# The first token tile of layer two built from a gather and a product of slots and tokens

## The chip, the cores and the metric

One core of one Trainium2 chip. The metric is the device time of one launch in microseconds; the time quoted for the kernel before is the median of three runs.

## What is computed

There are 4096 tokens (128 samples of 32 tokens) of 256 features. Layer one adds to `x` a mixture of four experts over a per-sample mixed input. Each expert takes its 1024 best tokens, runs a two-layer network over them, scales each row by its probability and adds it to that token's row. Layer two is a gated network with low-rank adapters that the sample's subject selects, followed by one more linear layer, again added to its input.

```python
# layer one (x_mixed = x @ cond_weights[subject])
for i in range(E):                                    # E = 4, capacity = 1024
    score = where(assigned_i, probs[:, i], -inf)
    sel_p, sel_idx = top_k(score, capacity)
    h = gelu(flat_x[sel_idx] @ W1[i])
    out = out.at[sel_idx].add(h @ W2[i] * p)          # scatter-add of rows
x = x + out
# layer two: y = x@W + (x@A[subject])@B[subject] for gate, up and down
h = silu(lora(x, Wg, Ag, Bg)) * lora(x, Wu, Au, Bu)
x = x + lora(h, Wd, Ad, Bd) @ (weight * scale).T + bias
```

## The kernel before

Every fp32 matrix is split into two fp32r parts, hi and lo, and a product is three matmuls (`product`, L1081 to L1083).

**Layer one** runs in 8 blocks of 512 slots, two blocks for each expert. A block has 8 steps of the hidden dimension. A step `s` is an up-product into `bank[s % 2]`, two gelus on ACT (`hid`, L564; `hf`, L567), one subtraction on DVE (`hid_lo`, L957) and, two steps later on PE, a down-product that accumulates the block's rows in PSUM. The last block, number 7, is cut into two parts of 256 slots, 8 steps each; its four quarters of 128 rows stand in banks 4 to 7. ACT scales the finished rows by the slot's probability (`rows_of_y`, L554) and POOL adds them to the token rows `x1_rows` in HBM by an indirect DMA with addition (`scatter`, L452), four for each block. A block's scatters wait for those of the block before.

**The order of layer two's tiles** is computed on chip: samples are sorted by subject so that each tile of 16 samples (512 tokens) needs two adapters. A product with `sample_id` and `goes_is` gives the order; DVE reads it in step LAST0+8 (`sample_rows`, L938 and L941), writing `sample_at` (the sample at each place) and `x1_row` (row numbers for the gathers) and raising `ids_in` to 5.

**Between the layers** stands the part that the change touches. PE finishes block 7 (`down(STEPS0 - 1, split=True)`), then runs 40 matmuls that nobody reads (`keep_busy(WAIT_X1, ...)`, L1175), and waits for the rows of tile 0. ACT splits off the first adapter pair's columns (`adapter_columns`, L597 and L600), then scales the last two quarters of block 7 and loads the Silu table. POOL scatters these quarters; when all scatters have landed (`scattered`), SP and ACT each read one quarter of tile 0 (`first_rows`, L341), and POOL the other two (`gather_x1(0)`, L480) and then tile 1. PE turns the four quarters of `x1_sb[0]` (L1344), ACT takes `x1s_hi` (L631), DVE `x1s_lo` (L999), and PE begins tile 0: eight matmuls that need the hi part only (L1352, L1353), the low-rank products (L1260, L1262), the rest of the first two hidden steps, and the adapter products (L1293).

**Layer two** then runs in 8 tiles of 512 tokens, 8 hidden steps each. In step 3 of each tile PE turns the rows of the next one (L1254). POOL gathers the adapter rows `b_pair` (L472) and the token rows, one tile or two ahead. The outputs are stored by SP.

Each engine has its own queue of instructions in program order. POOL's indirect DMAs share one DMA queue.

## Time and profile before

| what | value |
|---|---|
| median of three runs | 651.91 us (651.81 to 652.7) |
| the profiled execution's own time | 653.1 us |
| its span, first to last instruction | 651.3 us |
| PE, matmul busy | 605.0 us (93%) |
| PE weight load busy | 503.4 us (77%) |
| DVE busy | 382.1 us (59%) |
| ACT busy | 214.4 us (33%) |
| POOL busy | 132.6 us (20%) |
| mean granted clock of TensorE | 0.971 |

The engines are PE (TensorE matmul), PEld (its weight load), DVE (VectorE), ACT (ScalarE), POOL (GpSimd) and SP (SyncE). The span is what the trace covers. Layer one ends and layer two begins between 277 and 302 us of the span. A granted clock of 1.00 is the level of 2.4 GHz, 0.50 the level of 1.2 GHz.

### The profile page before, as it was taken

The page shows a single profiled execution, that of the slowest core. Times are in us where ns is not written, and L with a number is a line of the kernel's source. Part 1 is how long each engine was busy: PE and PEld are TensorE (multiplying, and loading weights), DVE is VectorE, ACT ScalarE, POOL GpSimd, SP SyncE. Part 2 cuts the span into 40 slices and gives each one's busy share as a digit, 9 for nine tenths or more (in the row PEclk, how much of TensorE's full clock was granted, in tenths as well). Part 3 has the DMA queues.
Part 4 walks back from the last instruction along what each step waited for, and adds up shares of the span by engine and source line. Part 5 has one row for each costly group of instructions (what it writes and reads, how often), then busy time and mean ns, then how long its engine had stood idle before and what let it go on. Part 6 is the DMA issues. An engine that isn't in the chain of part 4 may idle for free.

```text
span 651.3 us, 9696 instructions
## 1 busy us (share of the span) xinstructions
PE 605.0 (93%) x3323; PEld 503.4 (77%) x3323; DVE 382.1 (59%) x827; ACT 214.4 (33%) x448; POOL 132.6 (20%) x113
## 2 busy tenths in 40 slices
PE   4867389999999999979999999999999999999994
PEld 2735269999999999967888888888888888888883
DVE  7687867886786556505455545554555455545533
ACT  2435025764874755432212213122122131221110
POOL 4000040745453540652002003011030020000000
PEclk9979579999999999999999999999999999999997
DMA  8996329416329330831003104013031040120012
GB/s 309 318 334 234 106 87 365 65 36 192 34 78 295 42 49 9 195 70 45 0 1 117 21 1 126 13 41 96 2 117 21 0 125 12 45 61 2 13 21 33
DMA packets 64219, 60.74 MB, mean 93 GB/s; under 512 B 37424, under 2 KB 56624, under 8 KB 62832
## 3 DMA queue, kind: packets, MB, share of 16 engines
q1 hardware_dynamic: 53072, 38.04, 19.2%
q0 software_dynamic: 8736, 21.76, 13.5%
q10 hardware_dynamic: 2368, 0.39, 0.3%
q8 instruction: 23, 0.38, 0.2%
q14 instruction: 20, 0.16, 0.1%
HBM read 44.98 MB, written 19.40 MB: 99 GB/s over the span
## 4 chain that ended last, share of the span: by engine, by line
PE 86%; DVE 7%; DMA 2%; issue 1%; ACT 1%; POOL 0%; SPq 0%; ACTq 0%; DVEq 0%; POOLq 0%
PE bank L1081 23%; PE bank L1082 22%; PE bank L1083 22%; PE bank L1293 5%; PE bank L1262 3%; PE bank L1260 3%; DVE mix_row L668 2%; PE bank L1140 1%; PE bank L1114 1%; PE bank L1147 1%; PE bank L1194 1%; DVE onehot_r L831 1%; PE bank L1254 1%; DVE passed L780 1%; DVE passed_n L783 1%
## 5 line engine op out<-in xcount | busy, mean ns | idle before, releaser
L621 ACT ACTIVATE act<-bank 128x512 f32<-128x512 f32 x64 | 38.2, 598 | 229.9 <-PE bank L1293 229.9
L1046 DVE TENSOR_TENSOR prod<-bank,act 128x512 f32<-128x512 f32 x64 | 44.2, 690 | 99.6 <-PE bank L1293 99.6
L957 DVE TENSOR_TENSOR hid_lo<-hf,hid_hi 128x512 fp32r<-128x512 f32 (+1 forms) x72 | 45.4, 631 | 48.6 <-ACT hf L567 48.2
L1081 PE MATMUL bank<-w_hi,hid_hi 128*128 128x256 f32 x256 | 72.2, 282 | 0.0
L1082 PE MATMUL bank<-w_lo,hid_hi 128*128 128x256 f32 x256 | 72.1, 282 | 0.0
L1083 PE MATMUL bank<-w_hi,hid_lo 128*128 128x256 f32 x256 | 71.5, 279 | 0.0
L452 POOL DMA_INDIRECT x_rows<-y_sb,slot_row x32 | 53.7, 1678 | 65.9 <-ACT y_sb L554 58.9
L564 ACT ACTIVATE hid_hi<-bank 128x512 fp32r<-128x512 f32 (+1 forms) x72 | 39.8, 552 | 71.1 <-PE bank L1083 70.7
L472 POOL DMA_INDIRECT b_pair<-b_rows,b_row x8 | 8.5, 1059 | 238.2 <-PE bank L1312 237.6
L1081 PE MATMUL bank<-xs_hi,w_hi 128*128 128x512 f32 (+1 forms) x144 | 54.7, 380 | 0.0
L1082 PE MATMUL bank<-xs_lo,w_hi 128*128 128x512 f32 (+1 forms) x144 | 53.2, 370 | 0.0
L1083 PE MATMUL bank<-xs_hi,w_lo 128*128 128x512 f32 (+1 forms) x144 | 53.2, 370 | 0.0
L441 POOL DMA_INDIRECT xg<-flat_rows,slot_row x32 | 32.8, 1024 | 91.5 <-DVE slot_row L840 63.7
L1081 PE MATMUL bank<-x1s_hi,wg_hi 128*128 128x512 f32 x126 | 50.5, 401 | 0.9 <-DVE prod L1046 0.9
L1082 PE MATMUL bank<-hid_lo,wd_hi 128*128 128x512 f32 x128 | 50.8, 397 | 0.0
L1081 PE MATMUL bank<-hid_hi,wd_hi 128*128 128x512 f32 x128 | 50.6, 395 | 0.0
L1081 PEld LDWEIGHTS bank<-w_hi,hid_hi 128*128 128x128 f32 x256 | 48.1, 188 | 2.4
L1082 PEld LDWEIGHTS bank<-w_lo,hid_hi 128*128 128x128 f32 x256 | 48.1, 188 | 2.2
L1083 PE MATMUL bank<-hid_hi,wd_lo 128*128 128x512 f32 x128 | 49.8, 389 | 0.0
L1082 PE MATMUL bank<-x1s_lo,wg_hi 128*128 128x512 f32 x126 | 49.3, 392 | 0.0
L1083 PE MATMUL bank<-x1s_hi,wg_lo 128*128 128x512 f32 x126 | 49.2, 390 | 0.0
L1082 PE MATMUL bank<-x1s_lo,wu_hi 128*128 128x512 f32 x126 | 49.0, 389 | 0.0
(262 smaller groups left out, 1299.8 us busy)
## 6 DMA issues: line engine op xcount, KB each, us to landing
w_raw<-in_L_ffn_W SPq DMA_DIRECT2D x8, 1024.0 KB, 7.3
xT<-in_xT SPq DMA_DIRECT2D x8, 512.0 KB, 8.5
x_sb<-in_x SPq DMA_DIRECT2D x8, 512.0 KB, 8.7
flat_rows<-flat_st SPq DMA_DIRECT2D x8, 512.0 KB, 5.5
outT<-out_sb SPq DMA_DIRECT2D x120, 32.0 KB, 1.6
b_rows<-b_all_hi SPq DMA_DIRECT2D x1, 1152.0 KB, 9.4
b_rows<-b_all_lo SPq DMA_DIRECT2D x1, 1152.0 KB, 12.5
wdT<-in_wdT SPq DMA_DIRECT2D x1, 1024.0 KB, 5.3
```

The source lines that it names most:

```text
L441: pool.indirect_dma_start(out=xg[:, q, :], out_offset=None, in_=flat_rows[:, :], in_offset=bass.IndirectOffsetOnAxis(ap=slot_row[:, e, hal ...
L452: pool.indirect_dma_start(out=x1_rows[:, :], out_offset=bass.IndirectOffsetOnAxis(ap=slot_row[:, e, half * GB + q:half * GB + q + 1], axis=0),
L564: act.activation(hid[s % 4][0][:, n], bank[s % 2][:, n], ACT.Gelu)
L621: act.activation(act1[h % 2][:, :], bank[h % 2][:, :], ACT.Silu).then_inc(silu1, 1)
L957: dve.tensor_tensor(lo[:, n], hf[s % 2][:, n], hi[:, n].bitcast(f32), ALU.subtract).then_inc(hid0, 1)
L1046: dve.tensor_tensor(prod[h % 2][:, :], bank[2 + h % 2][:, :], act1[h % 2][:, :], ALU.mult).then_inc(prod1, 1)
L1081: pe.matmul(out, lh, rh, start=start, stop=False, skip_group_check=True)
L1082: pe.matmul(out, lh, rl, start=False, stop=False, skip_group_check=True)
L1083: return pe.matmul(out, ll, rh, start=False, stop=stop, skip_group_check=True)
L1260: pe.matmul(out[:, :], a_pair[par][:, i, :, :].rearrange("p a r -> p (a r)"), hi, start=start, stop=False, skip_group_check=True)
L1262: return pe.matmul(out[0:96, :], a_pair[par][:, i, 0:3, :].rearrange("p a r -> p (a r)"), lo, start=False, stop=stop, skip_group_check=True)
L1293: pe.matmul(out[:, :], b_pair[par][:, i * HID + h * P:i * HID + (h + 1) * P], u[:, :], start=False, stop=True, skip_group_check=True).then ...
```

## The change

Tile 0 of layer two is no longer read after all the scatters have landed. POOL gathers its rows earlier, into `x1_first`, when blocks 0 to 6 have landed, so without block 7. PE turns them between the last two down-products of layer one. Block 7's scaled rows are also kept on chip as hi and lo parts (`y_last`), and DVE writes a 0/1 matrix `pick` with one row for each slot of block 7 and one column for each token of tile 0: 1 where the slot holds that token. Sixteen matmuls of `y_last` with `pick` give block 7's share of tile 0, and DVE adds it to the turned rows. Block 7 is still scattered, for the tiles after the first. The adapter columns of tile 0 move into the last steps of layer one, the 40 matmuls and `first_rows` go, and the Silu table is loaded later.

```diff
@@ SBUF @@
+        x1_first, x1T_first = sb("x1_first", [P, GB, D], f32), sb("x1T_first", [P, KD, BT], f32)
+        first_id, slot_f = sb("first_id", [P, SB, 32], f32), sb("slot_f", [P, GB], f32)
...
+        pick = sb("pick", [P, GB, BT], f32r)
+        y_last = two("y_last", [P, GB, D])
@@ sync @@
-            first_rows(sp, 0)
@@ gpsimd @@
+            pool.wait_ge(ids_in, 5)
+            pool.wait_ge(xsT, KD * NB0)
+            pool.wait_ge(scattered, 16 * GB * (NB0 - 1))
+            for q in range(GB):
+                pool.indirect_dma_start(
+                    out=x1_first[:, q, :], out_offset=None, in_=x1_rows[:, :],
+                    in_offset=bass.IndirectOffsetOnAxis(ap=x1_row[:, q:q + 1], axis=0)).then_inc(first_in, 16)
             pool.wait_ge(b_out, 32)
             pool.wait_ge(packed_in, 1)
             for t in range(2):
                 gather_b(t)
+            pool.wait_ge(first_in, 16 * GB)
             scatter(NB0 - 1)
             pool.wait_ge(scattered, 16 * GB * NB0)
-            pool.wait_ge(ids_in, 5)
-            for t in range(2):
-                gather_x1(t)
+            gather_x1(1)
@@ scalar @@
+            def last_hi(q):
...
+                act.activation(y_last[0][:, q, :], y_at(NB0 - 1, q), ACT.Copy,
+                               scale=slot_p[:, E - 1, GB + q:GB + q + 1]).then_inc(y_hi, 1)
...
                 if h == 1 and part:
                     rows_of_y(b, (0, 1))
+                    for q in range(2):
+                        last_hi(q)
...
+                if s == LAST0 + KH + 3:
+                    act.wait_ge(packed_in, 1)
+                    act.wait_ge(lo1, len(SPLITS1))
+                    adapter_column(0, 0, 0)
+                if s == LAST0 + KH + 5:
+                    adapter_column(0, 0, 1).then_inc(a_in, 1)
...
-            act.wait_ge(lo1, len(SPLITS1))
-            adapter_columns(0, 0, (packed_in, 1))
+            for q in range(2, GB):
+                last_hi(q)
+            act.wait_ge(y_lo, GB)
             rows_of_y(NB0 - 1, (2, 3))
-            act.activation(warm[:, :], cols[:, 0:1], ACT.Silu)
-            first_rows(act, 1)
...
             for k in range(KD):
-                act.wait_ge(x1_t, k + 1)
-                act.activation(x1s[0][0][:, k, :], bank[4 + k][:, :], ACT.Copy).then_inc(x1_act, 1)
-            for k in range(KD):
-                act.wait_ge(x1_lo, k + 1)
-                act.activation(x1T[0][:, k, :], bank[4 + k][:, :], ACT.Copy)
+                act.wait_ge(x1_sum, k + 1)
+                act.activation(x1s[0][0][:, k, :], x1T[0][:, k, :], ACT.Copy).then_inc(x1_act, 1)
+            act.activation(warm[:, :], cols[:, 0:1], ACT.Silu)
@@ vector @@
+            def first_tokens():
+
+                dve.wait_ge(ids_in, 5)
+                dve.tensor_copy(slot_f[:, :], slot_row[:, E - 1, GB:2 * GB])
+                link(dve.scalar_tensor_tensor(first_id[:, :, :], over(sample_at[:, 0:SB], 32), 32.0,
+                                              iota[:, 0:32].unsqueeze(1).to_broadcast([P, SB, 32]), ALU.mult, ALU.add))
+
+            def picked(q):
+
+                dve.tensor_scalar(pick[:, q, :], first_id[:, :, :].rearrange("p s n -> p (s n)"), slot_f[:, q:q + 1], None,
+                                  ALU.is_equal).then_inc(pick_in, 1)
+
+            def last_lo(q):
+
+                dve.wait_ge(y_hi, q + 1)
+                dve.scalar_tensor_tensor(y_last[1][:, q, :], y_at(NB0 - 1, q), slot_p[:, E - 1, GB + q:GB + q + 1],
+                                         y_last[0][:, q, :].bitcast(f32), ALU.mult, ALU.subtract).then_inc(y_lo, 1)
...
+                if s == LAST0 + KH + 1:
+                    first_tokens()
+                if s in (LAST0 + KH + 2, LAST0 + KH + 3):
+                    for q in range(2):
+                        picked(2 * (s - LAST0 - KH - 2) + q)
+                if s == LAST0 + KH + 4:
+                    for q in range(2):
+                        last_lo(q)
...
             for k in range(KD):
-                x1_low(0, k + 1, k, bank[4 + k][:, :])
+                dve.wait_ge(x1_t, k + 1)
+                dve.tensor_copy(x1T_first[:, k, :], bank[2 + k][:, :]).then_inc(first_ev, 1)
+            for q in range(2, GB):
+                last_lo(q)
+            for k in range(KD):
+                dve.wait_ge(pick_mm, k + 1)
+                dve.tensor_tensor(x1T[0][:, k, :], bank[2 + k][:, :], x1T_first[:, k, :], ALU.add).then_inc(x1_sum, 1)
+            for k in range(KD):
+                x1_low(0, k + 1, k, x1T[0][:, k, :])
@@ tensor @@
             down(STEPS0 - 2)
+            pe.wait_ge(ids_in, 5)
+            pe.wait_ge(first_in, 16 * GB)
+            for k in range(KD):
+                for c in range(GB):
+                    last = pe.transpose(bank[2 + k][:, c * P:(c + 1) * P].bitcast(f32r),
+                                        x1_first[:, c, k * P:(k + 1) * P].bitcast(f32r), ident_r[:, :])
+                last.then_inc(x1_t, 1)
             down(STEPS0 - 1, split=True)
...
             pe.wait_ge(lo1, len(SPLITS1))
-            keep_busy(WAIT_X1, bank[0], wg)
-
-            for c in range(GB):
...
+            def from_last(k):
+
+                for q in range(GB):
+                    for j in range(2):
+                        q_, j_ = (q, j) if q < 2 else (2 + j, q - 2)
+                        if k == 0:
+                            pe.wait_ge(y_lo if j_ else y_hi, q_ + 1)
+                        last = pe.matmul(bank[2 + k][:, :], y_last[j_][:, q_, k * P:(k + 1) * P], pick[:, q_, :],
+                                         start=q == 0 and j == 0, stop=q == GB - 1 and j == 1, skip_group_check=True)
+                last.then_inc(pick_mm, 1)
+
+            pe.wait_ge(pick_in, GB)
+            pe.wait_ge(first_ev, KD)
+            for k in range(KD):
+                from_last(k)
```

## Rows read from the trace of the kernel before

**Rows 1.** Chain of waits that ended last, 262 to 302 us: start, us, what.
```profile
281.93 3.78 DMA x_rows<-y_sb,slot_row
...
287.92 2.86 DMA x_sb<-x_rows
...
291.69 0.61 ACT x1s_hi L631
```
**Rows 2.** Busy time of each engine by stretch; then PEclk, DMA share, GB/s.
```profile
288.00:290.80 2.80, 0.03 (x1) 0.00 (x0) 0.00 (x0) 0.00 (x0) 2.15 (x3) 1.00 0.63 171
...
292.30:296.20 3.90, 3.86 (x10) 2.99 (x11) 1.29 (x2) 1.67 (x3) 2.96 (x4) 0.56 0.36 101
...
301.00:303.30 2.30, 1.41 (x7) 0.85 (x6) 0.80 (x2) 1.08 (x2) 0.00 (x0) 1.00 0.00 0
```
**Rows 3.** Timeline of PE: start, us, instruction, [idle before <-releaser].
```profile
277.97 0.34 PE L1081 MATMUL bank<-w_hi,hid_hi 128*128 128x256 f32 x1
...
278.73 9.29 PE L1175 MATMUL bank<-wg_hi 128*128 128x512 f32 x40
...
295.62 0.63 PE L1260 MATMUL bank<-x1s_hi,a_pair 128*128 128x512 f32 x1
...
301.34 0.39 PE L1293 MATMUL bank<-ug,b_pair 128*128 128x512 f32 x1
...
313.48 0.46 PE L1254 MATMUL bank<-ident_r,x_sb 128*128 128x128 f32 x4
```
**Rows 4.** Timeline of POOL, scatters (L452) and gathers (L472, L480).
```profile
264.43 1.56 POOL L452 DMA_INDIRECT x_rows<-y_sb,slot_row  x1 [0.30 <-issue]
...
267.62 1.20 POOL L472 DMA_INDIRECT b_pair<-b_rows,b_row  x1 [0.30 <-issue]
...
285.98 1.02 POOL L480 DMA_INDIRECT x_sb<-x_rows,x_row  x1 [2.49 <-DMA x_rows<-y_sb,slot_row]
...
297.33 0.95 POOL L480 DMA_INDIRECT x_sb<-x_rows,x_row  x1 [0.30 <-issue]
```
**Rows 5.** DMA issues, 262 to 300 us: last number is median us to landing.
```profile
x_sb<-x_rows,x_row POOLq DMA_INDIRECT x10, 2.7
...
x_rows<-y_sb,slot_row POOLq DMA_INDIRECT x7, 3.8
b_pair<-b_rows,b_row POOLq DMA_INDIRECT x2, 7.2
```
**Rows 6.** Timeline of ACT in the last steps of layer one.
```profile
269.06 0.84 ACT L554 ACTIVATE y_sb<-bank,slot_p 128x256 f32<-128x256 f32 x2
...
275.33 0.39 ACT L564 ACTIVATE hid_hi<-bank 128x256 fp32r<-128x256 f32 x1 [0.75 <-PE bank L1083]
...
276.75 0.39 ACT L564 ACTIVATE hid_hi<-bank 128x256 fp32r<-128x256 f32 x1 [0.75 <-PE bank L1083]
277.03 0.38 ACT L567 ACTIVATE hf<-bank 128x256 f32<-128x256 f32 x1
277.67 0.68 ACT L597 ACTIVATE a_pair<-a_all_hi 128x576 fp32r x1 [0.27 <-issue]
...
280.18 1.28 ACT L606 ACT_TABLE_LOAD   x1
```
**Rows 7.** Timeline of DVE in the same steps.
```profile
268.11 1.08 DVE L941 TENSOR_SCALAR x_row<-bank,pack_f 32x32 int32<-32x32 f32 x4
...
277.44 0.42 DVE L957 TENSOR_TENSOR hid_lo<-hf,hid_hi 128x256 fp32r<-128x256 f32 x1 [0.99 <-ACT hf L567]
```
**Rows 8.** Groups by line and shape, DVE and ACT: count | busy, mean ns.
```profile
L1050 DVE CAST hid_hi<-prod 128x512 fp32r<-128x512 f32 x64 | 27.3, 427 | 2.9
...
L994 DVE TENSOR_TENSOR um<-bank,pack_f 128x512 f32<-128x512 f32 x16 | 11.1, 691 | 16.6 <-PE bank L1262 16.6
...
L1010 DVE SCALAR_TENSOR_TENSOR ug<-um_hi,pack_f,um 128x512 fp32r<-128x512 f32 x8 | 6.0, 752 | 0.3
...
L572 ACT ACTIVATE wg_hi<-wg_lo_raw 128x512 fp32r<-128x512 f32 x4 | 2.5, 634 | 0.0
```

## What the change should do to the time

> **What bounds the kernel now.** The chain of waits comes first, because it says what the end of the run hangs on between the layers. PE's work carries it up to the last scaled rows of layer one. Then it leaves PE: the last scatter of block 7 takes 3.78 us to land, the read of tile 0's rows 2.86 us more, ACT's hi part 0.61 us [rows 1]. The timeline of PE shows the same from the other side [rows 3]. The last down-product starts at 277.97, and the 40 matmuls that nobody reads run from 278.73 for 9.29 us, so until 288.0. Then the stretch table has PE at 0.03 of 2.80 us [rows 2], and the low-rank products of tile 0 start only at 295.62. From 277.97 to 295.62 are 17.65 us in which the only useful PE work is one down-product (six matmuls, 277.97 to 278.73, 0.76 us), eight transposes and eight matmuls. The idle stretch has a second price: the granted clock, at 1.00 until then, averages 0.56 from 292.30 to 296.20 [rows 2], so for most of these 3.9 us it is at the 1.2 GHz level. After 295.62 PE is the bound again, so what is gained here should arrive at the end one for one.
>
> **The change, part by part.** I follow the new path with the old times as anchors.
>
> *The early read.* It needs block 6's last scatter, issued at 264.43 [rows 4] and landed 3.8 us later [rows 5], at 268.2, and the row numbers, which DVE finishes at 268.11 + 1.08 = 269.2 [rows 7]. The ten L480 issues start 285.98 to 297.33, 1.26 us apart [rows 4]. So POOL issues the four gathers at 269.3, 270.6, 271.8 and 273.1, and with 2.7 us to landing [rows 5] the last is there at 275.8. With the 3.8 us of a scatter as the upper bound it is 276.9. PE wants them when it has done the last but one down-product, at 277.97. So the read costs nothing; its cover is PE's own work, with 1.1 to 2.2 us to spare. Past that, each microsecond costs one, because the last down-product is queued behind the wait.
>
> *What POOL does later.* The two `b_pair` gathers (before, the second started at 267.62 [rows 4]) now come after the four, at 274.4 and 275.7, and land 7.2 us later [rows 5], at about 283. The first adapter product wants them near 291.7. Then POOL waits for `first_in` (275.8 to 276.9, no real wait) and issues block 7's scatters. Such issues stand 1.56 + 0.30 = 1.9 us apart [rows 4]; the two last quarters now also wait for ACT, which takes them after `y_lo`, and go out at about 281.2 and 283.1, landing at 286.9. Tile 1's four gathers are issued from 287.0 and the last lands at 287.0 + 3 x 1.26 + 2.7 = 293.5. PE turned them at 313.48 [rows 3]; 9.6 us earlier is 303.9. This has 10 us of cover. SP loses `first_rows` and gains nothing.
>
> *ACT.* A step takes 1.42 us (275.33 to 276.75) and two gelus end 0.66 us after its start (276.75 to 277.41) [rows 6], so a step leaves 0.75 us. Two `last_hi` cost as much as the two scaled rows at 269.06, 0.84 us. An adapter column costs 0.27 us before it and 0.68 us for its hi copy [rows 6]; its smaller lo copy has no row here and takes no longer than the hi copy, so 1.0 to 1.6 us, and I take 1.1. Each of these three insertions makes the next gelu 0.3 to 1.0 us late, and the step after catches up, since they sit one or two steps apart. PE takes a step's hidden part two steps later, at which point it has about 1.2 us to spare. Zero, with at most 0.3 us left over at the last but one step.
>
> *DVE.* `first_id` has two broadcast inputs: 0.75 us, as L1010 [rows 8]. The four `picked` have no row of their own. They read one SBUF tile and write one of 512 columns. The nearest row is the cast L1050 with 0.43 us, the upper bound L1010 with 0.75 us [rows 8]. I take 0.45. Two in a step with the 0.42 us of `hid_lo` [rows 7] make 1.3 us, inside a step of 1.42. At 0.75 they make 1.9 us, twice, and PE would stand about 0.6 us. The Trainium skill, "VectorE: DVE Perf Modes", section "The perf-mode tier table", gives `tensor_scalar` on fp32 in SBUF twice the rate of a two-tensor operation, which agrees with L1050 against L1010 and would put the picks at the lower end.
>
> *The new path on PE.* Eight transposes: four take 0.46 us with their drain [rows 3], about 0.3 us each four when they follow each other, so 0.6 us, to 278.55. The last down-product, 0.76 us, to 279.3. DVE copies the turned rows out of PSUM from 278.5 on, two at the 0.69 us of L994 [rows 8], to 279.9, and PE waits for both: 0.6 us idle. The first four products need quarters 0 and 1, long done. ACT's hi parts of quarters 2 and 3 (0.42 us each, from 279.1) are there at 279.9, DVE's lo parts (0.45 each, from 279.9) at 280.8, before the seventh and eighth product ask for them at 281.3. Sixteen products at 9.29 / 40 = 0.23 us [rows 3] are 3.7 us, to 283.6, with the last result at 283.75. Then the sum for the second half on DVE 0.69 us, its hi part on ACT 0.63 us (from SBUF, as L572 [rows 8]), to 285.1, the lo part on DVE 0.69 us, to 285.8. With some 0.2 us for hand-overs the low-rank products start at 286.0. PE has its eight hi matmuls beside this: four from 283.6, four from 285.1, done at 286.0 too.
>
> *What is late next.* The low-rank start moves from 295.62 to 286.0, **9.6 us earlier**. The adapter pair's columns are ready at about 276. The Silu table (1.28 us [rows 6]) is loaded from 285.1 to 286.6, and the first Silu follows L1293, at 301.34 before and about 291.7 after. Nothing else lies between. The two first low-rank matmuls were still at the low clock, another 0.2 to 0.3 us, which I leave as a margin for hand-overs.
>
> *The clock.* PE's idle stretches become 0.6 us and 0.6 us. At 301.00 to 303.30 the kernel before has PE idle for 0.9 us with a granted clock of 1.00 [rows 2]; so I take full clock through the seam. That is part of the 9.6 us: in the stretch at 0.56 the ten matmuls filled 3.9 us [rows 2], and at 0.23 us each they would take 2.3.
>
> **The sum.** The span is 651.3 - 9.6 = 641.7 us. The profiled execution takes 1.8 us more than its span, 653.1, so 643.5 for it; against the median of the runs, 1.2 us under that execution, 651.91 - 9.6 = **642.3 us**.
>
> **The rivals.**
> 1. *The first rows come late* (13%), because DVE's new work holds up POOL's issues. The picks fall at 272 to 274, over the last two gathers. If each pick stopped POOL for its own 0.45 us, four would move the last landing by 1.8 us, to 277.6, and with the 3.8 us of a scatter [rows 5] to 278.7: 0.7 us of stall. With picks of 0.75 us it is 279.9 and 1.9 us of stall. So 643.0 to 644.2. For it: one `b_pair` issue took 1.20 us [rows 4] while DVE wrote the row numbers from 268.11 on [rows 7]. Against it: the gather issued at 297.33 took 0.95 us. The Trainium skill, "SBUF — State Buffer", section "Who interferes with whom", speaks for this rival: it says that a DVE cast or `tensor_scalar` in a two-port mode and GpSimd lock each other out for a whole instruction, so that a DMA from the GpSimd queue waits for its descriptors. No row here shows such a wait alone.
> 2. *The clock falls for a while* (10%). With the 40 matmuls gone, PE's work from 279 to 286 is broken by waits. Half clock over a stretch like the one before, 3.9 us at 0.56, costs 2 us: 644.3.
> 3. *DVE or ACT falls behind in the last steps* (5%): the picks at 0.75 us and the adapter columns at the wrong moment, 0.6 to 1 us: 643.1.
> 4. *Slower than before* (2%): the clock falls and does not come back while PE's work is in pieces. Each microsecond at 1.2 GHz costs half. It eats the whole gain from 19 us at half clock on, and makes the kernel measurably slower from 22 us on; low from 280 to 305 gives 642.3 + 12.5 = 654.8. Against it: it came back within 4 us before [rows 2], behind a longer pause.
> 5. *It doesn't do what it says* (2%): the read waits for block 7 somehow, or the rows land at 287 and PE's last down-product behind them: near 651.9.
>
> **How the numbers follow.** The forecast has 68%. It covers 641.5 (copies and sums faster than L994 says, up to 0.8 us) to 643.2 (picks at the upper bound, some hand-overs). The range of 641.3 to 644.8 adds rivals 2 and 3 and most of 1. A change under 0.2%, 1.3 us, can't be told from none. Faster by more: 0.96, all cases but 4 and 5; within 0.2%: 0.02; slower: 0.02.
>
> **What would show it.** In the profile after: L1175 with WAIT_X1 gone; the transposes of `x1_first` straight behind the last but one down-product, without an idle time released by a DMA; the sixteen products starting near 279.9 at 0.23 us each; the low-rank products near 286.0; PEclk at 1.00 from 278 to 292; tile 1's turn without a wait on a DMA. The prediction is wrong if PE waits for `x1_first` for over a microsecond, if the stretch 279 to 292 has a clock under 0.9, or if the shift at L1293 is not found at the end of the span.

## The result, and the profile after

The changed kernel ran in five of seven jobs; a job is a row of runs on one chip, with runs of the kernel before among them. What the change gives depends on the job. The distance in the table is from the start of the row-number product (L1302 after, in step LAST0+8) to the first adapter product (L1357 after, L1293 before, [rows 3]), in the job's profile. It leaves out what lies ahead of the change, where single executions of any kernel here differ by up to 3 us.

| job | changed, us | before, us | ratio, 95% | distance, us |
|---|---|---|---|---|
| 1 | 647.68 (645.59 to 648.58) | 652.32 | 0.9913 (0.9895 to 0.993) | 29.60 |
| 3 | 643.05 (642.69 to 643.34) | 652.18 | 0.9859 (0.9833 to 0.9884) | 26.80 |
| 4 | 643.39 (642.39 to 644.24) | 654.13 | 0.9834 (0.9814 to 0.9854) | 26.02 |
| 5 | 642.75 (642.43 to 644.79) | 653.26 | 0.9853 (0.9823 to 0.9883) | 26.07 |
| 6 | 643.71 (643.4 to 644.3) | 652.28 | 0.9862 (0.9825 to 0.9899) | 26.04 |

Before, the distance was 35.50. The forecast was 642.3 in a range of 641.3 to 644.8. Job 1, the measurement that it was made for, lies 5.4 us above the forecast and 2.9 us outside its range: half of the gain came. In jobs 3 to 6 all 16 executions are inside. The document has to explain two things: why jobs 3 to 6 came out as they did, and where 4.5 us went in job 1.

**The ordinary profile** is that of job 6 (span 641.6 us). Timeline of PE, start, us, instruction, [idle before <-releaser], as in [rows 3]:

```profile
266.19 0.23 PE L1302 MATMUL bank<-goes_is,sample_id 128*128 128x128 bf16 x1
...
278.32 0.81 PE L1308 MATMUL bank<-ident_r,x_first 128*128 128x128 f32 x8
278.96 0.35 PE L1138 MATMUL bank<-w_hi,hid_hi 128*128 128x256 f32 x1
...
280.36 0.47 PE L1410 MATMUL bank<-pick,y_last_hi 128*128 128x512 f32 x1 [0.46 <-DVE x1T_first L1112]
...
284.09 0.39 PE L1422 MATMUL bank<-x1s_hi,wg_hi 128*128 128x512 f32 x1
...
285.70 0.50 PE L1422 MATMUL bank<-x1s_hi,wg_hi 128*128 128x512 f32 x1 [0.54 <-ACT x1s_hi L656]
...
286.73 0.40 PE L1324 MATMUL bank<-x1s_hi,a_pair 128*128 128x512 f32 x1
```

The turned rows follow the last but one down-product without a pause, the sixteen products start 2.0 us later, and PE stands only twice, for half a microsecond each. The stretch table ([rows 2] has its columns) shows the clock at its upper level throughout, over the 6.4 us of the seam too:

```profile
278.00:280.30 2.30, 1.90 (x19) 1.69 (x17) 1.71 (x4) 0.72 (x2) 2.00 (x2) 1.00 0.98 409
280.30:286.70 6.40, 5.80 (x24) 4.54 (x25) 3.34 (x6) 3.26 (x6) 4.38 (x3) 1.00 1.04 266
286.70:292.00 5.30, 5.30 (x25) 4.21 (x24) 3.65 (x6) 0.45 (x2) 2.43 (x3) 1.00 0.20 45
```

**The profile of job 1** (span 645.6 us), the same timeline:

```profile
277.38 0.28 PE L1140 MATMUL bank<-xs_hi,w_lo 128*128 128x256 f32 x1
...
278.09 0.28 PE L1140 MATMUL bank<-w_hi,hid_lo 128*128 128x256 f32 x1
281.44 0.39 PE L1138 MATMUL bank<-w_hi,hid_hi 128*128 128x256 f32 x1 [3.07 <-issue]
...
284.32 0.47 PE L1410 MATMUL bank<-pick,y_last_hi 128*128 128x512 f32 x1 [0.43 <-DVE x1T_first L1112]
```

PE stands for 3.07 us before a down-product. Its operand was late, and ACT's timeline shows why the operand was:

```profile
273.77 0.39 ACT L587 ACTIVATE hid_hi<-bank 128x256 fp32r<-128x256 f32 x1
...
275.98 0.39 ACT L587 ACTIVATE hid_hi<-bank 128x256 fp32r<-128x256 f32 x1 [1.54 <-PE bank L1140]
...
277.20 0.35 ACT L578 ACTIVATE a_pair<-a_all_lo 128x192 fp32r x1
280.27 0.38 ACT L587 ACTIVATE hid_hi<-bank 128x256 fp32r<-128x256 f32 x1 [2.72 <-remote]
...
281.75 0.38 ACT L587 ACTIVATE hid_hi<-bank 128x256 fp32r<-128x256 f32 x1 [0.82 <-remote]
```

ACT had nothing to do and waited for up-products that PE had long dispatched. The last matmul of the up-products started at 272.97, 274.38, 275.79 and 277.38. In the steps just before them the semaphore rises 0.29 us after such a start. For these four it rises at 273.75, 275.95, 280.25 and 281.73: 0.5, 1.3, 4.2 and 4.1 us later than that. ACT's and DVE's own signals came at once. The profile can't name what ACT waited for, hence "remote"; the chain of waits has the same gap:

```profile
277.20 0.35 ACT a_pair L578
277.55 2.69 another core or an unknown queue
...
280.93 0.80 another core or an unknown queue
```

I call this late signals. The profile of job 1 also lacks some 770 of about 6460 semaphore records.

The last block is not the only place. The same profile has the same signal late in the first step of two earlier blocks, near 135 and 159 us, long before the burst, the early reads, the adapter columns or the matrices. PE and ACT in job 1:

```profile
133.10 0.98 PE L1240 MATMUL bank<-slotted,onehot_r 128*128 128x48 bf16 x32
...
135.17 0.39 PE L1140 MATMUL bank<-xs_hi,w_lo 128*128 128x512 f32 x1
...
137.03 0.60 ACT L587 ACTIVATE hid_hi<-bank 128x512 fp32r<-128x512 f32 x1 [2.45 <-PE bank L1140]
```

and in job 6:

```profile
134.76 0.39 PE L1140 MATMUL bank<-xs_hi,w_lo 128*128 128x512 f32 x1
...
135.19 0.60 ACT L587 ACTIVATE hid_hi<-bank 128x512 fp32r<-128x512 f32 x1 [1.02 <-PE bank L1140]
```

From matmul to gelu it is 1.86 us in job 1 and 0.43 in job 6. PE did not stand there, so this lateness of 1.4 us cost nothing.

### The profile page after: what moved, and what is told of

It is laid out like the page before. It is cut to its first block, busy times and chain, and to the rows that moved or that the text cites. A ratio compares the mean times of both kernels' runs of the same rounds, so it can differ in the third digit from the quotient of the medians.

```text
span 645.6 us, 9619 instructions
## 1 busy us (share of the span) xinstructions
PE 599.7 (93%) x3299; PEld 498.4 (77%) x3299; DVE 388.9 (60%) x841; ACT 214.9 (33%) x450; POOL 134.9 (21%) x115
## 4 chain that ended last, share of the span: by engine, by line
PE 87%; DVE 5%; DMA 2%; issue 1%; ACT 1%; SPq 1%; another core or an unknown queue 1%; POOL 0%; DVEq 0%; ACTq 0%; POOLq 0%
PE bank L1138 23%; PE bank L1139 23%; PE bank L1140 23%; PE bank L1357 5%; PE bank L1326 3%; PE bank L1324 3%; DMA xT<-in_xT 2%; PE bank L1197 1%; PE bank L1171 1%; PE bank L1204 1%; PE bank L1251 1%; DVE onehot_r L854 1%; SPq L363 1%; PE bank L1318 1%; PE bank L1410 1%
## 5 line engine op out<-in xcount | busy, mean ns | idle before, releaser
L452 POOL DMA_INDIRECT x_rows<-y_sb,slot_row x32 | 53.7, 1679 | 62.5 <-ACT y_sb L560 54.9
L472 POOL DMA_INDIRECT b_pair<-b_rows,b_row x8 | 8.2, 1022 | 229.7 <-PE bank L1376 229.1
L1138 PE MATMUL bank<-x1s_hi,wu_hi 128*128 128x512 f32 x126 | 49.0, 389 | 0.0
```

The costliest lines, as they stand in the source:

```text
L452: pool.indirect_dma_start(out=x1_rows[:, :], out_offset=bass.IndirectOffsetOnAxis(ap=slot_row[:, e, half * GB + q:half * GB + q + 1], axis=0),
L1138: pe.matmul(out, lh, rh, start=start, stop=False, skip_group_check=True)
```

## The experiments

Theory 1: the burst of the two `b_pair` gathers (2.36 MB, now issued behind the early reads, 276 to 285 us) falls on layer one's last steps and stalls them. Theory 2: ACT's adapter columns do it. Theory 3: DVE's matrices do. Theory 4: PE's fetch of instructions is held up. After the first runs came theories 5 (transfers and new work together), 6 (the early reads) and 7 (the recording of the execution).

**Job 2: four edits of the changed kernel.**

> POOL issues the two b_pair gathers ahead of the four early reads of x1_first, as it did in the kernel before; nothing else is changed. In the changed kernel PE stands from 278.1 to 281.4 us and again for 1 us behind the gelus of the last two steps, and ACT waits there for signals of PE that come 0.5 to 4 us after PE's own stamps. Theory 1 (the 2.36 MB of b_pair, which now flow from 276 to 284 us, hold up PE's last steps or its signals): the burst ends near 277, the idle 3.07 us goes, and the time falls by 3 to 4 us, to 643.5 to 645. Theory 2 (ACT's adapter columns with their register loads): unchanged at 647.4, stall at the same step. Theory 3 (DVE's picks and lo rows): unchanged. Theory 4 (the block of instructions that PE fetches at 280.6 is held up behind the transfers): falls as under theory 1, with the fetch back at about 277. A new cost in all of them: the early read starts one to two us later if the gathers ahead of it wait.

```diff
+            pool.wait_ge(b_out, 32)
+            pool.wait_ge(packed_in, 1)
+            for t in range(2):
+                gather_b(t)
             pool.wait_ge(ids_in, 5)
...
-            pool.wait_ge(b_out, 32)
-            pool.wait_ge(packed_in, 1)
-            for t in range(2):
-                gather_b(t)
```

> ACT makes the first adapter pair's columns behind the last scaled rows, as before, and no longer between the gelus of layer one's last steps. Theory 2 (the columns with their register loads hold up ACT and with it PE): the idle 3.07 us of PE goes, and the columns lie beside PE's products after 284, so 643.5 to 645. Theories 1 and 4 (transfers): the stall stays at 278 to 281.5, the time at 647.4 within 1 us. Theory 3 (DVE): also unchanged.

```diff
-                if s == LAST0 + KH + 3:
...
-                    adapter_column(0, 0, 0)
-                if s == LAST0 + KH + 5:
-                    adapter_column(0, 0, 1).then_inc(a_in, 1)
...
             for q in range(2, GB):
                 last_hi(q)
+            act.wait_ge(lo1, len(SPLITS1))
+            adapter_columns(0, 0, (packed_in, 1))
```

> DVE makes the four 0/1 matrices and the first two lo parts of the last block's rows behind the copies of the turned rows, no longer between the hidden parts of the last steps. That puts 4 x 0.45 us + 2 x 0.45 us on the path to the sixteen products, 2.5 to 2.7 us. Theory 3 (DVE's work inside the steps makes the stall of 4 us): the idle time of PE at 278 goes and the time is 646 to 647, about the same as the changed kernel. Theories 1, 2 and 4: the stall stays and the time is 649.5 to 650.5.

```diff
-                if s in (LAST0 + KH + 2, LAST0 + KH + 3):
...
-                        last_lo(q)
...
+            for q in range(GB):
+                picked(q)
-            for q in range(2, GB):
+            for q in range(GB):
                 last_lo(q)
```

> POOL issues the two b_pair gathers behind the scatters of the last block, at about 284 us instead of 275.7, so no burst lies over layer one's last steps; its data are needed by the adapter product near 296 us. Theories 1 and 4 (transfers over the last steps): PE's idle 3.07 us at 278 goes, the seam is done near 286, and the adapter products then wait for b_pair (landing near 292 to 293), so 643.5 to 646. Theories 2 and 3 (ACT's or DVE's new work in the steps): the stall stays and the time is 647.4 or more.

```diff
-            pool.wait_ge(b_out, 32)
-            pool.wait_ge(packed_in, 1)
-            for t in range(2):
-                gather_b(t)
             pool.wait_ge(first_in, 16 * GB)
             scatter(NB0 - 1)
+            pool.wait_ge(b_out, 32)
+            pool.wait_ge(packed_in, 1)
+            for t in range(2):
+                gather_b(t)
             pool.wait_ge(scattered, 16 * GB * NB0)
```

| kernel, job 2 | us | ratio, 95% | distance, us |
|---|---|---|---|
| `b_pair` first | 644.71 (643.44 to 646.35) | 0.9858 (0.9829 to 0.9886) | 26.96 |
| columns late | 647.39 (646.93 to 647.79) | 0.9906 (0.9878 to 0.9933) | 30.40 |
| picks late | 650.79 (649.13 to 651.89) | 0.9961 (0.9946 to 0.9977) | 33.28 |
| `b_pair` last | 644.16 (643.36 to 647.11) | 0.987 (0.9832 to 0.9907) | 26.81 |

The changed kernel did not run in this job; the measure is its 29.60 us of job 1. With the burst moved away, to either side, the 3 us go. With ACT's or DVE's work moved away they stay: theories 2 and 3, as the sole cause, fall. PE's and ACT's rows with `b_pair` last:

```profile
275.04 0.39 ACT L587 ACTIVATE hid_hi<-bank 128x256 fp32r<-128x256 f32 x1 [1.56 <-PE bank L1140]
...
277.68 0.38 PE L1138 MATMUL bank<-w_hi,hid_hi 128*128 128x256 f32 x1 [0.25 <-DVE hid_lo L998]
```

The signals still begin to be late at the same step, by up to 1.35 us, but they recover at once. Theory 4 falls by the kernel with the columns late: PE's block of instructions is fetched at 275.9 there (276.2 in the kernel before), and ACT's longest wait comes after it:

```profile
279.30 0.38 ACT L587 ACTIVATE hid_hi<-bank 128x256 fp32r<-128x256 f32 x1 [2.30 <-remote]
```

In that kernel, and in the one with the picks late, the clock fell behind the stall, which is my rival 2 as a follower of something else. With the columns late the sixteen products then take 5.17 us (282.45 to 287.62) instead of 3.73 (stretch table, columns late):

```profile
278.00:280.00 2.00, 1.21 (x13) 1.06 (x11) 0.01 (x1) 0.66 (x2) 1.70 (x2) 1.00 1.04 410
280.00:282.00 2.00, 0.97 (x6) 0.77 (x6) 1.51 (x3) 0.84 (x2) 0.54 (x1) 1.00 0.94 327
282.00:284.00 2.00, 1.55 (x4) 1.29 (x5) 0.98 (x3) 1.59 (x4) 0.00 (x0) 0.51 1.04 279
```

**Job 3: parts alone in the kernel before, and the changed kernel again.**

> This is the kernel before with POOL's order of the changed kernel alone: four early reads of x1_first (into a tile that nobody reads), then the two b_pair gathers, then block 7's scatters. ACT, DVE and PE do what they did. The changed kernel's stall over the last steps is measured by the signals of PE: they come 0.3 us behind the last matmul's start until 272 us and 0.5 to 4.2 us late after it. Theory 1 (the transfers alone do it): PE's last down-products are 3 to 4 us late, as in the changed kernel, and the time is 655 to 656.5. Theory 5 (only the transfers together with the new work of ACT and DVE in the same steps): PE runs through its last steps without idle time, and the time is 653 to 654, the 1 us being the later scatters.

> The kernel before with the two b_pair gathers issued when PE has done all but three down-products of layer one, near 275 us, between the two halves of block 7's scatters, so that the burst of 2.36 MB lies where the changed kernel has it; there are no early reads. Theory 1 in its narrow form (the burst over the last two steps does it, whoever else is at work): PE stands for 2 to 4 us before its last two down-products, 655 to 656.5. Theory 4 (a fetch of instructions, which PE makes at 276.2 us in the kernel before, is held up behind the burst): the same, with the fetch seen 2 to 4 us later. Theory 6 (the early reads are needed for the stall): no idle time on PE, at most 1 us from scatters that go out beside the burst, 652 to 654.

```diff
                 for q in range(GB):
+                    if b == NB0 - 1 and q == 2:
+                        pool.wait_ge(b_out, 32)
+                        pool.wait_ge(packed_in, 1)
+                        pool.wait_ge(down0, STEPS0 - 3)
+                        for t in range(2):
+                            gather_b(t)
                     pool.wait_ge(y_out, GB * b + q + 1)
```

> The changed kernel with the b_pair gathers behind the scatters, and with DVE's 0/1 matrices and first lo parts and ACT's adapter columns all taken out of the last steps, so that of the change only the early reads and ACT's two hi parts are left in them. There PE's signals were still up to 1.35 us late with the b_pair gathers alone taken away. If that rest comes from ACT's and DVE's new work, PE's signals are on time (0.3 us) and the last down-product but one starts 0.7 us earlier; if it comes from the early reads, the lateness stays. Either way the 2.7 us of DVE's work now lie on the path: 646 to 647.5, against 644.2 with them in the steps.

> The changed kernel itself once more, beside the others. If the stall is a property of the program, PE stands again for 3 us before its last down-product but one and ACT's last two hidden parts wait for PE's signals; the distance from the start of the row-number product to the first adapter product is 29.6 us again (35.5 in the kernel before), and the time 646.5 to 648.5. If it was one execution's accident, the distance is near 27 us.

The first kernel takes POOL's lines of the change as they stand, the third joins the edits of three kernels above. Measured: reads in the kernel before 656.8 us (654.33 to 658.94), 1.0069 (1.0048 to 1.009); burst late 655.79 (654.9 to 658.66), 1.006 (1.0032 to 1.0088); steps free 646.98 (645.9 to 647.99), 0.9916 (0.9886 to 0.9945), distance 29.24; the changed kernel 643.05, distance 26.80. The two edits of the kernel before have distances of 38.29 and 37.98, against 35.50.

Nobody's signals were late in this job. Theory 1 as I had put it falls here: the changed kernel has its burst in the same place and no stall. Both edits of the kernel before are slower, but not by PE's steps, in which ACT's idle time stays at 0.67 to 0.75 us. By the time alone theory 1 (655 to 656.5) would have seemed right for both. They are slower since tile 0 waits there for block 7's scatters, and these are now issued behind or beside the burst. Timeline of POOL with the burst late, the last scatter and what waited for it:

```profile
281.36 1.57 POOL L458 DMA_INDIRECT x_rows<-y_sb,slot_row  x1 [0.30 <-issue]
287.37 1.02 POOL L486 DMA_INDIRECT x_sb<-x_rows,x_row  x1 [4.45 <-DMA x_rows<-y_sb,slot_row]
```

The chain of waits has its landing:

```profile
281.36 5.76 DMA x_rows<-y_sb,slot_row
```

That is 5.76 us, against 3.78 in [rows 1]. With the early reads the last scatter is issued 1.4 us later and lands in 4.09 us. The rest of the 2.8 and 2.5 us of distance goes with the clock, which is at 0.50 for 6.8 us behind the wait in both and for 3.4 us in the kernel before. The medians are 4.6 and 3.6 us slower; what lies beyond the distance I have not traced. So the changed order of POOL is bearable only with the rest of the change.

In the changed kernel PE waited for the first rows in this job. It turns them 12.82 us behind the row-number product, in job 6 12.13 us behind it, and these 0.69 us are nearly all of the difference between 26.80 and 26.04:

```profile
278.18 0.86 PE L1308 MATMUL bank<-ident_r,x_first 128*128 128x128 f32 x8 [0.53 <-DMA x_first<-x_rows,x_row]
```

The chain of waits shows why: the last of the four reads took 4.87 us from issue to landing, where I had taken 2.7 and at most 3.8.

```profile
273.18 4.87 DMA x_first<-x_rows,x_row
```

**Job 4: side by side, on the chip of job 2.**

> The changed kernel a third time, as the measure for the three beside it. Its two profiles so far differ: in one PE's signals to ACT came up to 4.2 us late over the last steps of layer one, PE stood for 3 us, and the runs gave 645.6 to 648.6; in the other, taken on another chip, they were on time and the runs gave 642.7 to 643.3. If the lateness belongs to the chip, this run and the three beside it show one of the two throughout; if it belongs to the single execution, the runs of one kernel scatter between 643 and 648.

> The two b_pair gathers behind the last block's scatters, as in an earlier run, now beside the changed kernel on the same chip. Where PE's signals are late, the theory that the b_pair burst stretches the lateness says 3 us less than the changed kernel beside it, with at most 1.4 us of lateness left. Where they are on time, the two kernels are within 1 us.

> As the kernel beside it with the b_pair gathers last, and with DVE's 0/1 matrices and first lo parts and ACT's adapter columns out of the last steps. It pays 2.7 us for that. If the late signals come from the work of ACT and DVE in these steps, they are on time here and late in the other three; if from the early reads, they are late by up to 1.4 us here too; where the chip shows no lateness at all, the distance from the row-number product to the first adapter product is 29.2 us again.

> The kernel with the b_pair gathers last, its four early reads left out: x1_first is filled with zeros by one instruction on POOL in their place, so the first tile lacks what the rows would bring. ACT's and DVE's new work stays in the steps. If the early reads make PE's signals late, they are on time here where the others show lateness, 0.7 to 1 us less than the kernel with the reads; if ACT's and DVE's work does, the lateness stays. Without any lateness on this chip the time is that of the kernel with the b_pair gathers last, less the half microsecond that PE waited for the rows.

```diff
-            for q in range(GB):
-                pool.indirect_dma_start(
-                    out=x1_first[:, q, :], out_offset=None, in_=x1_rows[:, :],
-                    in_offset=bass.IndirectOffsetOnAxis(ap=x1_row[:, q:q + 1], axis=0)).then_inc(first_in, 16)
+            pool.memset(x1_first[:, :, :], 0.0).then_inc(first_in, 1)
...
-            pe.wait_ge(first_in, 16 * GB)
+            pe.wait_ge(first_in, 1)
```

The kernel without the reads is made from the one with `b_pair` last. It leaves out what the rows bring to tile 0.

| kernel, job 4 | us | ratio, 95% | distance, us |
|---|---|---|---|
| changed | 643.39 (642.39 to 644.24) | 0.9834 (0.9814 to 0.9854) | 26.02 |
| `b_pair` last | 643.23 (642.4 to 643.92) | 0.9832 (0.9813 to 0.9851) | 26.82 |
| steps free | 645.4 (644.8 to 648.35) | 0.988 (0.9848 to 0.9912) | 29.14 |
| no reads | 643.55 (642.74 to 645.25) | 0.985 (0.9828 to 0.9872) | 26.02 |

No late signals again, so the lateness isn't a property of that chip, and the place of the burst makes no difference here (in this profile the kernel with `b_pair` last had PE waiting 0.40 us for the rows). The kernel without the reads has the distance of the changed one to the hundredth: where the rows land in time the early reads cost nothing, as the sum said. Against `b_pair` last, from which it differs by the reads alone, its distance is 0.80 us shorter, which is the wait for the rows (its last read took 4.74 us to land); the medians don't show it (643.55 against 643.23). Whether the reads bring the lateness it can't tell.

**Jobs 5 and 6: two more tries for the late signals, and what the moved work costs without them.**

> The changed kernel a fourth time. If the late signals come with the job (whatever the chip is doing at that time) they are either in the profile and in all timed runs, 646 to 648.5, or in none, 642.4 to 644.3. If each execution draws them anew, the runs scatter over both.

> The changed kernel with the b_pair gathers last and with DVE's matrices and first lo parts and ACT's adapter columns out of the last steps. In two jobs without late signals it took 2.0 and 3.9 us more than the changed kernel beside it. Should the signals be late in this job: if ACT's and DVE's work in the steps brings the lateness, this kernel has none and is level with or ahead of the changed kernel; if the early reads bring it, it is late too and stays 2 us or more behind.

> The changed kernel once more, as the measure for the two beside it: 642.4 to 644.3 with PE's signals on time, 646 to 648.5 with them late, the same of the two in all three kernels.

> ACT's first adapter columns behind the last two hi parts instead of between the gelus. They take 2.1 us there, before the scaled rows of the last two quarters, so block 7's last scatters go out some 2 us later, with cover. If the insertions between the gelus were free, as I forecast, this kernel is no faster than the changed one: 642.5 to 644. If each made PE wait a little, it is 0.3 to 0.8 us faster.

> DVE's four 0/1 matrices and first two lo parts behind the copies of the turned rows. 4 x 0.45 and 2 x 0.45 us less the waits that they fill: 2.0 to 2.7 us more than the changed kernel beside it, if they cost nothing inside the steps. In exchange POOL's third and fourth early read are issued in 0.95 us each instead of 1.1 to 1.2, so that the rows land 0.3 to 0.5 us earlier; if that lock was what PE waited for, the kernel wins that back and is 1.6 to 2.2 us behind.

| kernel | us | ratio, 95% | distance, us |
|---|---|---|---|
| job 5, changed | 642.75 (642.43 to 644.79) | 0.9853 (0.9823 to 0.9883) | 26.07 |
| job 5, steps free | 646.61 (645.09 to 648.57) | 0.9894 (0.9866 to 0.9922) | 29.26 |
| job 6, changed | 643.71 (643.4 to 644.3) | 0.9862 (0.9825 to 0.9899) | 26.04 |
| job 6, columns late | 643.08 (642.95 to 644.08) | 0.9854 (0.9817 to 0.9892) | 26.06 |
| job 6, picks late | 645.46 (645.23 to 647.32) | 0.9893 (0.9852 to 0.9934) | 29.28 |

Signals were on time in all five. ACT's columns between the gelus cost 0.02 us, none. DVE's work costs 3.2 us by the distance when it stands on the path, where I had expected 2.7 at most. Only 1.7 of them are DVE's: the products start 15.86 us behind the row-number product instead of 14.17. The other 1.5 are the clock's. PE pauses for 2.17 us before the products, the clock falls to 0.50 for 3.4 us, and the sixteen products take 5.28 us (281.05 to 286.33) instead of 3.73 (280.36 to 284.09). Timeline of PE and stretch table, picks late:

```profile
281.05 0.76 PE L1406 MATMUL bank<-pick,y_last_hi 128*128 128x512 f32 x1 [2.17 <-DVE pick L976]
...
286.33 0.39 PE L1418 MATMUL bank<-x1s_hi,wg_hi 128*128 128x512 f32 x1
```

```profile
280.90:284.30 3.40, 3.25 (x8) 2.61 (x9) 1.61 (x5) 0.84 (x2) 1.00 (x1) 0.50 0.94 247
```

The kernel with free steps has the same 3.4 us at 0.50 in each of its three jobs. So my rival 2 is real wherever DVE's work stands on the path, with late signals or without.

Four kernels ran in jobs of both kinds and have a pair of distances: the changed kernel 29.60 with late signals and 26.05 without, columns late 30.40 and 26.06, picks late 33.28 and 29.28, `b_pair` last 26.81 and 26.82 (the second with PE's wait for the rows). Late signals cost 3.6 to 4.3 us with the burst behind the reads; of the 4.3, 1.4 are the fallen clock. With the burst elsewhere they cost at most 0.9 us (26.81 and 26.96 against 26.05).

**Job 7: more records.**

> The changed kernel with 7 x 60 waits on SP that are satisfied at once, spread over the last eight steps of layer one; each leaves records in the profile and touches no data, no queue of a transfer and no other engine. Theory 7 (the recording of the execution holds PE up where records come too densely): PE's signals come late over these steps and semaphore records are missing, as in the first two jobs; the distance from the row-number product to the first adapter product grows from 26.05 to 27 to 30 us, and the time to 644 to 648. If the recording isn't the cause, or bears this load too, the distance stays at 26.0 to 26.8 and the time at 642.4 to 644.3; that would not clear it, since the load may be too small.

```diff
                 sp.dma_start(b_rows[i * P:(i + 1) * P, :], part[:, 0, :].bitcast(f32)).then_inc(b_out, 16)
+            for k in range(7):
+                sp.wait_ge(down0, STEPS0 - 8 + k)
+                for _ in range(60):
+                    sp.wait_ge(ids_in, 1)
```

Measured: 648.54 us (648.35 to 649.55), 0.9927 (0.9898 to 0.9956), distance 31.97, with PE's signals late and ACT waiting as in job 1:

```profile
274.74 0.38 ACT L592 ACTIVATE hid_hi<-bank 128x256 fp32r<-128x256 f32 x1 [1.57 <-PE bank L1145]
...
281.36 0.38 ACT L592 ACTIVATE hid_hi<-bank 128x256 fp32r<-128x256 f32 x1 [2.78 <-remote]
```

The numbers are those of theory 7, and yet they don't prove it. The profile has 5593 semaphore records, and some are missing long before the first added wait (268.4 us), as in jobs 1 and 2. So this job was one with late signals anyway, and no changed kernel without the waits ran beside it. The distance, 31.97 against 29.60 in job 1, also holds a clock of 0.50 for 3.4 us, and the profile has only 210 of the 420 waits, none of them between 271.7 and 279.9 us. What speaks for theory 7 is the lateness itself. Near 135 and 159 us, where no wait is added, it is 1.5 to 1.6 us, as in jobs 1 and 2 (1.4 to 1.6). In the first late step of the last block it is 2.0 us, where the five profiles of jobs 1 and 2 have 0.5 to 0.7. That is one profile, and it shows at most that the added waits make the lateness larger.

**What is shown, and what stays open.** Shown: the 3 to 4 us need both the late signals and the burst in that place. Shown too: the signals don't need the change to be late. In all six profiles of jobs 1, 2 and 7 they are 1.4 to 1.6 us later than the usual 0.41 us near 135 and 159 us, in steps where nothing of the change runs, and in none of the 13 profiles of jobs 3 to 6. Both steps follow 32 small matmuls of L1240, issued 0.03 us apart; a third such group, at 109 us, has no late signal behind it. Open: what makes the signals late. In the last block they are late from the same step on, 6.4 us behind the row-number product, in five of the six; with the columns late it is one step later, so ACT's work there may have a share. Jobs 2, 4 and 7 ran on one chip, so it isn't the chip alone. They go with missing semaphore records: 5587 to 5684 are left in those six, 6391 or more in the other 13. The timed runs are slow together with the profiled one, but every time here is of an execution that is recorded, so the recording is not cleared. The Trainium skill, "NOTIFIC — the notification-queue block", section "7.1 Overflow: three behaviours, one of which stalls the engine", says that the block which writes such records holds its producers back inside rather than lose one; by that PE could be held up by its own records. No run here separates it. Theories 5 and 6 fall as the origin of the lateness, since it appears over 100 us ahead of the reads and of the new work. Whether these make it larger in the last block was not tested: neither the kernel without the reads, nor that with free steps, nor the two edits of the kernel before ran in a job with late signals. The kernel before took 652.3, 652.7 and 653.4 us in jobs 1, 2 and 7, no more than elsewhere.

## Why the prediction was right or wrong

Point by point in the profile of job 6. Its row-number product starts at 266.19, that of before at 265.83, so 0.36 us are added to each forecast time.

- **Early read.** Issues forecast from 269.7 to 273.5; measured:

```profile
269.81 1.08 POOL L489 DMA_INDIRECT x_first<-x_rows,x_row  x1 [3.46 <-DVE x_row L964]
271.19 0.97 POOL L489 DMA_INDIRECT x_first<-x_rows,x_row  x1 [0.30 <-issue]
272.47 1.23 POOL L489 DMA_INDIRECT x_first<-x_rows,x_row  x1 [0.30 <-issue]
274.00 1.14 POOL L489 DMA_INDIRECT x_first<-x_rows,x_row  x1 [0.30 <-issue]
275.45 0.94 POOL L472 DMA_INDIRECT b_pair<-b_rows,b_row  x1 [0.30 <-issue]
```

The last is 0.5 us later than forecast. PE turns the rows at 278.32 without a wait, the forecast's 277.97 + 0.36. In two of the five profiles of jobs 3 to 6 that have the reads and the rest of the steps as changed (job 3, and `b_pair` last in job 4) it waits 0.53 and 0.40 us. Right in the rest, with a smaller margin than I gave it: a landing of 2.7 us was the term that was too small, with 4.87 and 4.74 us in those two profiles, past my upper bound of 3.8.
- **Rival 1, DVE holds up POOL.** Right in kind, wrong in size: the rows did come late in those two profiles, by 0.7 and 0.6 us, and mostly by the landing. With the picks moved, in job 6, the third and fourth issue are shorter:

```profile
271.47 0.95 POOL L489 DMA_INDIRECT x_first<-x_rows,x_row  x1 [0.30 <-issue]
272.72 0.94 POOL L489 DMA_INDIRECT x_first<-x_rows,x_row  x1 [0.30 <-issue]
```

Four picks hold POOL up for 0.28 + 0.20 = 0.48 us in all, not for 4 x 0.45 = 1.8. The Trainium skill, "SBUF — State Buffer", section "Who interferes with whom", says that such a DVE instruction and GpSimd lock each other out for a whole instruction. If POOL stood for the whole of every pick it would be 1.8 us; the measured 0.48 decides here.
- **ACT.** Forecast zero; measured zero (26.06 against 26.04), where PE's signals are on time. Two of its gelus start with only 0.41 and 0.70 us of idle time, where there were 0.75: it falls behind and catches up.
- **DVE.** Two picks take 0.88 us, 0.44 each (forecast 0.45); `first_id` 0.69 (0.75). No wait.
- **The new path.** Products at 280.36 (forecast 279.9 + 0.36 = 280.3), sixteen at 0.23 us (280.36 to 284.09), DVE's sum 0.69, ACT's part 0.63, low-rank products at 286.73 (286.0 + 0.36 = 286.4). The missing 0.3 us are hand-overs. From there to L1357 it is 5.49 us instead of 5.72: the 0.2 us at full clock that I had left as a margin.
- **Sum.** 35.50 - 26.04 = 9.46 us up to L1357. To the end of the span it is 10.0 us (before 651.29 - 265.83 = 385.45, after 641.60 - 266.19 = 375.41), the last 0.6 us spread over layer two. Forecast 9.6.
- **The clock.** 1.00 through the seam, as forecast. Rival 2 showed in seven profiles of edits, at 0.50 for 3.4 us each time: columns late and picks late in job 2, the kernel of job 7, steps free in jobs 3 to 5 and picks late in job 6.
- **Tile 1.** Its gathers start at 288.96, not at 287.4: the last scatter is issued at 283.74, beside the burst, and the gather that waits for it starts 5.2 us later. Before it was 4.05 us (281.93 to 285.98), and I had taken 3.9, from the landing in [rows 5]. PE turns the rows at 304.36, without a wait (forecast 303.9 + 0.36 = 304.3). The cover held.

**The step that failed for job 1** is the premise under "ACT: zero" and under "its cover is PE's own work": that PE hands each step over as in [rows 6], with its signal right behind its matmuls. None of my cases had a signal of PE as what comes late. And I costed the `b_pair` gathers only by when they land (needed near 291.7), not by what they do to the steps under which they flow. In job 1 these two together took 3.6 us of distance, 29.60 against 26.04. With a start of the seam 0.4 us later (266.61 against 266.19) that is the whole 4.0 us between the spans of the two profiles, 645.6 and 641.6. The medians are 4.0 to 4.9 us apart.

Rival 3 did not come: ACT and DVE kept up, and in job 1 it was they who waited. Nor did 4 and 5: the clock of the changed kernel is 1.00 from 270 to 300 us in all five of its profiles, and the rows never waited for block 7.

## What to carry to other kernels

When a transfer is moved, look at the steps under which it flows, and not only at its deadline: behind the scatters the two gathers cost nothing in one kind of job (643.23 against 643.39) and saved some 3.5 us in the other (644.16 against 647.68, in two jobs), so that version is the safer of the two. Measure a change in more than one job before explaining it: job 1's 4.6 us and the 8.6 to 10.7 us of jobs 3 to 6 are the same program. And compare from a mark just ahead of the change: the distance repeats to 0.05 us in three of four profiles, while whole executions scatter by over 2. Last, read the clock of an edit before its time is put down to the work that was moved: of the 3.2 us that DVE's work seemed to cost, 1.5 were the clock's.

## What the runs showed of the hardware that I had not expected

PE's semaphore signals came up to 4.2 us later than usual behind its matmuls in job 1, and 5.7 us in the kernel with the picks late (281.40, for a matmul that started at 275.44). Several then came within 0.15 us of each other (275.02, 275.09 and 275.17 with `b_pair` last), where 1.4 us of matmuls lie between the first and the last. That points to work that was done and a message that was held, which no run shows directly. An indirect DMA with addition took 3.8 us to land with the queue quiet. From its issue to the gather that waits for it were 4.05 us then, 5.1 to 6.5 us in the four profiles of the changed kernel with the signals on time, with the `b_pair` burst beside it. In job 1 PE stood 3.07 us and the clock stayed at 1.00; in job 2, with shorter pauses in a row, it fell to 0.51, and in job 6 one pause of 2.17 us came with the same fall.
